# Second block's attention: norms in groups of two tiles, the second half's projections inside the scan, the MLP's norm later

## The chip, the cores and the metric

The kernel runs on one core of one Trainium2 chip. The metric is the device time of one execution in microseconds, lower is better. The core has a matrix engine (TensorE, PE in the profile; its weight loads are PEld), three engines for elementwise work (VectorE is DVE, ScalarE is ACT, GpSimd is POOL) and SyncE (SP), which issues transfers. Each works through its own list of instructions in order and waits on semaphores for the others.

## The reference

Two transformer blocks over x of shape (4, 1024, 256) in float32. Each is "modulated norm, attention, add; modulated norm, feed-forward, add". Block 0 has softmax attention over full rows of 1024 and a low-rank feed-forward; block 1 has the part that the change touches, a causal linear attention with its own MLP inside, and then a mixture layer:

```python
h = _layernorm(x) * (1 + ca) + sa
x = x + ga * _L1_attn_ref(h, ...)      # below
h = _layernorm(x) * (1 + cb) + sb
x = x + gb * _L1_ffn_ref(h, ...)       # 16 tokens share 64 slots

def _L1_attn_ref(inputs, ...):         # 16 heads of 16
    x = layer_norm(inputs, ln1_scale, ln1_bias)
    q, k, v = x @ wq, x @ wk, x @ wv
    phi_q, phi_k = relu(q) + 1e-3, relu(k) + 1e-3
    kv  = cumsum_j(phi_k v^T)          # causal prefix sums
    num, den = phi_q . kv, phi_q . cumsum(phi_k)
    x = (num / den) @ wo + inputs
    y = layer_norm(x, ln2_scale, ln2_bias)
    return x + gelu(y @ w1 + b1) @ w2 + b2
```

## The kernel before

The four sequences are done one after the other by `batch(b, carry)`: four passes of the same instructions. In a pass the 1024 tokens are T = 8 tiles of 128 rows, in two halves of TH = 4 tiles. Nearly all products are float32.

There is no scheduler. Each engine has a `Lane`; `lane.do(emit, *after)` appends a step to that engine's list and notes which steps of other lanes it waits for. So **the order in which the Python code calls `do` is the order on each engine**, and an engine stands still while the next step of its list waits.

The eight PSUM banks go round in `Banks`: `take()` hands out the next bank with the step that last read it, and whoever writes the bank waits for that reader. During block 1's attention one bank (`state_bank`) is set aside and the other seven rotate.

The work around the change, in the order of the code at the end of `batch`:

1. `head_output` ends block 0's attention; `norm_stats` and `norm_apply` normalise each half of x.
2. `feed_rank`, `feed_wide`, `feed_rank2`, `feed_output` are block 0's feed-forward, both halves interleaved.
3. `attention_norms(half, ...)` is a generator with four pieces: statistics of x (L280 to L284), modulation into h (L995, L997), statistics of h, and the apply into xn (L288).
4. `turn` transposes a half (4 tiles by 2 column blocks) on TensorE, and ScalarE copies it out with scale and bias (L411, L418, L420).
5. `attention_inputs` makes keys and values (`wkv1`), queries (`wq1`) and the transposed keys kT of a half; `phi` is L1107 on VectorE; `split_queries` (L1139, ScalarE) writes q_par.
6. The scan runs over t = 0 to 7: `tile_scores` (L1154 on TensorE, then four masks `am` at L1163 on VectorE, 128x512 each), `tile_numerators` (L1181 and, from the second tile, L1185 with kv_state), `tile_state` (L1201, then kv_state at L1209) and `tile_outputs` (L1221, then rec at L1226 and y at L1228).
7. `attention_output(half)` turns y, multiplies by wo, adds to h (L1242), normalises it for the MLP, and leaves three additions and products per tile to GpSimd (L1247 to L1250). Then come `mlp_turn`, `mlp_wide`, `mlp_output`, and the mixture layer (`slot_turn`, `choices`, `chosen_rows`).

A norm of a half is four pairs of bn_stats and bn_aggr, one addition of eps for the four tiles (L283), one power of -1/2 on GpSimd for the four (L284) and four applies (L288) on VectorE.

## Time and profile before

| | |
|---|---|
| three runs | 2003.45, 2004.32, 2004.73 us; median 2004.32 |
| the profiled execution | 2002.16 us |
| its span | 2000.6 us |
| mean granted TensorE clock | 0.959 of full speed |
| busy: PE, DVE, ACT, POOL | 91%, 63%, 44%, 33% |

The span is about four equal passes of some 490 us; the four repeat each other's waits to 0.1 us. The part of a pass that the change touches takes about 120 us. The second pass has it between 771 and 893 us of the span (block 0's norms from 771, the scan from 832 to 893) and the mixture layer's norms up to 970 us. All rows below are of this pass. A granted clock of 1.00 is 2.4 GHz and 0.50 is 1.2 GHz.

### The profile page before, as it was taken

Reading aid. Unit: us, or ns where it says so; the run is one execution under the profiler, and the core shown is the slowest. Engines: PE = TensorE matmul, PEld = TensorE weight load, DVE = VectorE, ACT = ScalarE, POOL = GpSimd, SP = SyncE. Lnnn points to the kernel's source line nnn. Section 1 sums busy time; section 2 is a strip of 40 time slices with the busy share of each in tenths; the row PEclk is TensorE's granted clock in tenths of the full one; section 3 lists DMA queues with packets and bytes.
Section 4 is the critical chain, followed back from the end, with each engine's and each line's share of the span. In section 5 each row is a group of like instructions: output and inputs, shape, how many; then the busy total and the mean of one; then the engine's idle time right before and its main releaser. Section 6 shows DMA issues by size and latency. Waiting matters only on the chain. (4 is left out here: it accounts for less than half of the span.)

```text
span 2000.6 us, 41155 instructions
## 1 busy us (share of the span) xinstructions
PE 1815.9 (91%) x16401; PEld 1287.2 (64%) x16401; DVE 1266.0 (63%) x2699; ACT 887.4 (44%) x1934; POOL 660.6 (33%) x1010
## 2 busy tenths in 40 slices
PE   6999998898999989889899998988989999889888
PEld 4666675656666667566756666756775666765667
DVE  4687846634688883753468887464456888656435
ACT  4566623222467662322257665322135666432222
POOL 2455530120055552012115555201212555420220
PEclk9899998998999999899899999989989999999998
DMA  8566540040266563013136656203114666520400
GB/s 217 124 152 156 138 134 1 2 84 27 77 148 145 140 139 111 1 23 63 33 97 148 144 138 141 85 1 57 29 33 122 142 146 139 118 84 1 85 1 23
DMA packets 128558, 182.64 MB, mean 91 GB/s; under 512 B 33296, under 2 KB 89328, under 8 KB 127344
## 3 DMA queue, kind: packets, MB, share of 16 engines
q1 hardware_dynamic: 114928, 173.72, 36.2%
q10 hardware_dynamic: 13440, 6.30, 1.1%
q8 instruction: 131, 2.15, 0.5%
q14 instruction: 59, 0.48, 0.1%
HBM read 62.44 MB, written 4.24 MB: 33 GB/s over the span
## 5 line engine op out<-in xcount | busy, mean ns | idle before, releaser
L848 ACT ACTIVATE prob<-prob,neg_max 128x768 f32<-128x768 f32 (+5 forms) x384 | 273.8, 715 | 98.4 <-DVE neg_max L740 98.3
L643 PEld LDWEIGHTS bank<-placed,v_t 128*64 128x64 f32 x4608 | 251.2, 137 | 77.7 <-issue 77.7
L623 PE MATMUL scores<-k_t,q_t 64*128 64x128 f32 (+10 forms) x2176 | 291.3, 414 | 0.0
L643 PE MATMUL bank<-placed,v_t 128*64 128x128 f32 x4608 | 274.1, 275 | 17.2 <-DMA placed<-prob 9.7
L284 POOL TENSOR_TENSOR rstd<-rstd,minus_half 128x4 f32<-128x4 f32 x48 | 48.6, 1014 | 713.9 <-DVE rstd L283 713.9
L748 DVE STREAM_TRANSPOSE prob<-prob 128x1536 f32<-128x1536 f32 x128 | 223.7, 1768 | 24.3 <-ACT prob L848 24.0
L810 POOL COPY placed<-prob 32x768 f32<-32x768 f32 x256 | 210.8, 823 | 19.6
L623 PEld LDWEIGHTS scores<-k_t,q_t 64*128 64x128 f32 x2176 | 167.3, 190 | 73.4 <-issue 58.6
L740 DVE CUSTOM_DVE_ANT_1 prob<-scores,hx 128x128 f32<-128x128 f32 (+4 forms) x320 | 166.2, 579 | 59.7 <-PE scores L623 52.3
L797 POOL COPY rec_wide<-rec 128x128 f32<-128x128 f32 x256 | 65.4, 291 | 337.3 <-DVE rec L752 244.3
L848 ACT ACTIVATE hx<-hx,neg_max 128x896 f32<-128x896 f32 (+1 forms) x128 | 119.6, 935 | 83.5 <-DVE neg_max L740 82.8
L740 DVE CUSTOM_DVE_ANT_1 hx<-scores,hx 128x896 f32<-128x896 f32 (+1 forms) x128 | 114.8, 953 | 54.3 <-POOL placed L810 39.6
L748 DVE STREAM_TRANSPOSE hx<-hx 128x1536 f32<-128x1536 f32 x64 | 110.6, 1761 | 13.2 <-ACT hx L848 13.2
L957 DVE TENSOR_TENSOR tmp<-scores,mod_rows 128x256 f32<-128x256 f32 x71 | 30.1, 424 | 125.0 <-PE scores L430 119.1
L810 POOL COPY placed<-hx 32x768 f32<-32x768 f32 x128 | 105.5, 824 | 9.7
L684 PE MATMUL bank<-hT,w_ring 128*128 128x512 f32 x224 | 103.6, 605 | 0.0
L430 PE MATMUL scores<-wout,yT 128*128 128x256 f32 x384 | 90.0, 393 | 7.9 <-POOL yT L819 5.9
L430 PEld LDWEIGHTS scores<-wout,yT 128*128 128x128 f32 x384 | 74.0, 196 | 20.3 <-issue 10.2
L988 ACT ACTIVATE hid<-scores,b 128x512 f32<-128x512 f32 x92 | 60.0, 697 | 52.1 <-PE scores L439 52.1
L1163 DVE TENSOR_TENSOR am<-scores,tril 128x512 f32<-128x512 f32 x96 | 60.2, 683 | 32.2 <-PE bank L1154 19.7
L819 POOL TENSOR_TENSOR yT<-yT,tmp 128x256 f32<-128x256 f32 (+1 forms) x64 | 46.0, 730 | 103.3 <-ACT yT L861 103.3
L740 DVE CUSTOM_DVE_ANT_0 prob<-scores,hx 128x1024 f32<-128x1024 f32 x64 | 75.8, 1222 | 6.6 <-PE scores L623 6.6
(232 smaller groups left out, 3344.8 us busy)
## 6 DMA issues: line engine op xcount, KB each, us to landing
placed<-prob SPq DMA_DIRECT2D x768, 96.0 KB, 2.2
placed<-hx SPq DMA_DIRECT2D x384, 96.0 KB, 2.2
f<-in_L_ffn_f SPq DMA_DIRECT2D x16, 2048.0 KB, 13.5
x<-in_L_attn_x SPq DMA_DIRECT2D x8, 512.0 KB, 4.4
mod_rows<-mod_scratch SPq DMA_DIRECT2D x32, 128.0 KB, 5.7
out<-x SPq DMA_DIRECT2D x16, 256.0 KB, 2.2
w_ring<-in_L_attn_w_q ACTq DMA_DIRECT2D x24, 128.0 KB, 2.5
w_ring<-in_L_attn_w_kv_up ACTq DMA_DIRECT2D x48, 64.0 KB, 2.1
```

Source lines behind the costliest of these rows:

```text
L284: return pool.do(lambda e: nc.gpsimd.tensor_tensor(rstd[:, ts], rstd[:, ts], minus_half[:, ts], op=ALU.pow), var, filled)
L430: last = nc.tensor.matmul(ps, w, m, start=n == 0, stop=n == len(pieces) - 1)
L623: last = nc.tensor.matmul(score_tiles[head][:, at_ // 512, at_ % 512:at_ % 512 + count], q_t[buf][rows_, tile * P:(tile + 1) * P], k_of[bu ...
L643: last = nc.tensor.matmul(out_bank[rows_, at_:at_ + P], v_t[pair % 2][:, j, rows_], placed[m % 2][:, :, head, first_block(m, i) + j, :], s ...
L684: last = nc.tensor.matmul(ps, ring[:, c * P:(c + 1) * P], hT[:, c, cols], start=c == 0, stop=c == C - 1)
L740: nc.vector.tensor_tensor_reduce(prob[m % 3][:, :, head, blocks, :].rearrange("p g n i -> p g (n i)"), src.rearrange("p (g m) -> p g m", g ...
L748: nc.vector.transpose(p_, p_).then_inc(flow["shuffled"], 1)
L797: last = nc.gpsimd.tensor_copy(rec_wide[:, out_slot(m, tile), :].rearrange("p (a n) -> p a n", a=HEADS), rec[:, at_:at_ + HEADS].unsqueeze ...
L810: nc.gpsimd.tensor_copy(placed[m % 2][rows_, g, :, :, :], prob[m % 3][rows_, g, :, :, :]).then_inc(flow["kept"], 1)
L848: nc.scalar.activation(p_, p_, ACT.Exp, scale=-1.0, bias=neg_max[:, k:k + 1], accum_out=row_sum[:, k:k + 1]).then_inc(flow["exp_done"], 1)
L988: return lambda m, cols, ps, done: act.do(lambda e: nc.scalar.activation(dst[:, m, cols], ps, ACT.Gelu_apprx_tanh, bias=bias[:, m:m + 1]), ...
L1163: masked.append(dve.do(lambda e, r=r, ps=ps: nc.vector.tensor_tensor(am[t % 2][:, r * 4:r * 4 + 4, :], ps.rearrange("p (h n) -> p h n", h= ...
```

## The change

**Norms in groups of two.** `norm_stats` now ends each pair of tiles with its own addition and power, and returns for each tile the step that its apply waits for. Every norm of the kernel gets this: one addition and one power of 128x2 more, in place of one of 128x4.

**Turns tile by tile.** `turn` takes both banks first and transposes tile after tile into both, each waiting for its own tile; both copies of ScalarE wait for the last tile.

**The projections.** `attention_inputs` is split: `attention_queries`, `attention_keys` (two tiles) and `attention_keys_turned` (the kT of those two tiles, one bank, one copy). The first half does queries first, then keys 0 and 1, their turn, keys 2 and 3, their turn. The second half's turn and queries come at t = 2, keys 4 and 5 at its end, keys 6 and 7 at t = 3. The fill of v_tok's ones goes from VectorE to GpSimd.

**The second half's norms.** The modulation is now four applies on VectorE (into h) and eight products and additions on GpSimd; statistics of h stand between the masks of tiles 0 and 1, the applies after the masks of tile 1.

**The MLP's norm of the first half.** Its statistics are made in two pieces, at the ends of t = 5 and t = 6, and its applies at the end of t = 6, behind the masks of tile 7, just ahead of `mlp_turn`.

```diff
-        last = None
-        for t, r in zip(tiles or tiles_of(half), ready):
-            s = dve.do(lambda e, t=t: nc.vector.bn_stats(stats[:, t, :], src[:, t, :]), r)
-            last = dve.do(lambda e, t=t: nc.vector.bn_aggr(mv[:, t, :], stats[:, t, :]), s)
-        ts = slice(half * TH, (half + 1) * TH)
-        var = dve.do(lambda e: nc.vector.tensor_scalar(rstd[:, ts], mv[:, ts, 1], eps, None, op0=ALU.add), last)
-        return pool.do(lambda e: nc.gpsimd.tensor_tensor(rstd[:, ts], rstd[:, ts], minus_half[:, ts], op=ALU.pow),
-                       var, filled)
-
-    def norm_apply(src, half, inv, dve=dve):
-        return [dve.do(lambda e, t=t: nc.vector.tensor_scalar(
-            xn[:, t, :], src[:, t, :], mv[:, t, 0:1], rstd[:, t:t + 1], op0=ALU.subtract, op1=ALU.mult), inv)
-            for t in tiles_of(half)]
+        tiles = list(tiles or tiles_of(half))
+        inv = {}
+        for pair, ready_ in zip(zip(tiles[0::2], tiles[1::2]), zip(ready[0::2], ready[1::2])):
+            for t, r in zip(pair, ready_):
+                s = dve.do(lambda e, t=t: nc.vector.bn_stats(stats[:, t, :], src[:, t, :]), r)
+                last = dve.do(lambda e, t=t: nc.vector.bn_aggr(mv[:, t, :], stats[:, t, :]), s)
+            ts = slice(pair[0], pair[1] + 1, pair[1] - pair[0])
+            var = dve.do(lambda e, ts=ts: nc.vector.tensor_scalar(rstd[:, ts], mv[:, ts, 1], eps, None, op0=ALU.add), last)
+            step = pool.do(lambda e, ts=ts: nc.gpsimd.tensor_tensor(rstd[:, ts], rstd[:, ts], minus_half[:, ts], op=ALU.pow),
+                           var, filled)
+            inv.update({t: step for t in pair})
+        return inv
+
+    def norm_apply(src, half, inv, dve=dve, dst=None):
+        dst = xn if dst is None else dst
+        steps = {t: dve.do(lambda e, t=t: nc.vector.tensor_scalar(
+            dst[:, t, :], src[:, t, :], mv[:, t, 0:1], rstd[:, t:t + 1], op0=ALU.subtract, op1=ALU.mult), step)
+            for t, step in inv.items()}
+        return [steps[t] for t in tiles_of(half)]
...
-            copies = []
-            for c in range(C):
-                i, ps, reader = banks.take()
-
-                def transposes(e, c=c, ps=ps):
-                    for t in range(TH):
-                        last = nc.tensor.transpose(ps[:, t * P:(t + 1) * P], src[:, half * TH + t, c * P:(c + 1) * P],
-                                                   ident[:, :])
-                    return last
-
-                done = pe.do(transposes, *ready, reader)
+            copies, taken = [], [banks.take() for c in range(C)]
+            readers = [reader for i, ps, reader in taken]
+
+            def transposes(e, t):
+                for c, (i, ps, reader) in enumerate(taken):
+                    last = nc.tensor.transpose(ps[:, t * P:(t + 1) * P], src[:, half * TH + t, c * P:(c + 1) * P], ident[:, :])
+                return last
+
+            for t in range(TH):
+                done = pe.do(lambda e, t=t: transposes(e, t), ready[t], *readers)
+            for c, (i, ps, reader) in enumerate(taken):
...
-                    h[:, t, :], x[:, t, :], mv[:, t, 0:1], scale, op0=ALU.subtract, op1=ALU.mult), inv)
+                    h[:, t, :], x[:, t, :], mv[:, t, 0:1], scale, op0=ALU.subtract, op1=ALU.mult), inv[t])
...
-            h_done = modulated_rows(half, inv, mod_rows[:, 3, :], mod_rows[:, 2, :])
+            if half == 0:
+                h_done = modulated_rows(half, inv, mod_rows[:, 3, :], mod_rows[:, 2, :])
+            else:
+                h_done = []
+                for t, step in zip(tiles_of(half), norm_apply(x, half, inv, dst=h)):
+                    step = pool.do(lambda e, t=t: nc.gpsimd.tensor_tensor(h[:, t, :], h[:, t, :], mod_rows[:, 3, :],
+                                                                          op=ALU.mult), step, ROWS)
+                    h_done.append(pool.do(lambda e, t=t: nc.gpsimd.tensor_tensor(h[:, t, :], h[:, t, :], mod_rows[:, 2, :],
+                                                                                 op=ALU.add), step))
...
-        def attention_inputs(half, turned, between=iter(())):
-
-
-            if half == 0:
-                ones_set.append(dve.do(lambda e: nc.vector.memset(v_tok[:, :, :, HD1:VPAD], 1.0), turned[0]))
+        def attention_queries(half, turned):
+            q_done[half] = blocks(C, lambda m, cols: [(wq1[:, c, m * P:(m + 1) * P], nT[:, c, cols]) for c in range(C)],
+                                  half, P, lambda m, cols, ps, done: dve.do(phi(qT[:, m, cols], ps), done), turned=turned)
+            return split_queries(half)
+
+        def attention_keys(first, turned):
+
-            for t in tiles_of(half):
+            for t in (first, first + 1):
...
-                next(between, None)
-            q_done[half] = blocks(C, lambda m, cols: [(wq1[:, c, m * P:(m + 1) * P], nT[:, c, cols]) for c in range(C)],
-                                  half, P, lambda m, cols, ps, done: dve.do(phi(qT[:, m, cols], ps), done), turned=turned)
-            kT_done[half] = turn(k_tok, half, k_done, kT)
+            return k_done
+
+        def attention_keys_turned(first, k_done):
+            i, ps, reader = banks.take()
+
+            def transposes(e, t):
+                for c in range(C):
+                    at_ = (c * 2 + t - first) * P
+                    last = nc.tensor.transpose(ps[:, at_:at_ + P], k_tok[:, t, c * P:(c + 1) * P], ident[:, :])
+                return last
+
+            for t, k_step in zip((first, first + 1), k_done):
+                done = pe.do(lambda e, t=t: transposes(e, t), k_step, reader)
+            copy = act.do(lambda e: nc.scalar.copy(kT[:, :, first * P:(first + 2) * P],
+                                                   ps.rearrange("p (c n) -> p c n", c=C)), done)
+            banks.read_by(i, copy)
+            kT_done[first] = kT_done[first + 1] = copy
...
-            half, tok = t // TH, slice(t * P, (t + 1) * P)
+            tok = slice(t * P, (t + 1) * P)
...
-                             kT_done[half][c])
+                             kT_done[t])
...
-        def attention_output(half):
+        def attention_sum(half):
...
-            normed = normalise(h, half, wrote, EPS_LN)
+            return wrote
+
+        def attention_normed(half, inv):
+
+            normed = norm_apply(h, half, inv)
...
+        ones_set.append(pool.do(lambda e: nc.gpsimd.memset(v_tok[:, :, :, HD1:VPAD], 1.0), *rank2_1))
-        attention_inputs(0, attention_turn(0, attn_norm), islice(norms, 2))
-        split = {0: split_queries(0)}
+        attn_turned = attention_turn(0, attn_norm)
+        split = {0: attention_queries(0, attn_turned)}
+        k_first = attention_keys(0, attn_turned)
+        attention_keys_turned(0, k_first)
+        k_first = attention_keys(2, attn_turned)
+        next(norms)
+        attention_keys_turned(2, k_first)
-        attn_norm = next(norms)
+        next(norms)
-            if t + 3 == TH:
-                attn_turned = attention_turn(1, attn_norm)
-            if t + 2 == TH:
-                attention_inputs(1, attn_turned)
-                split[1] = split_queries(1)
+            if t == 2:
+                attn_turned = attention_turn(1, attn_norm)
+            if t == 3:
+                k_first = attention_keys(6, attn_turned)
+                attention_keys_turned(6, k_first)
+            if t == 2:
+                split[1] = attention_queries(1, attn_turned)
+            if t == 0:
+                attn_norm = next(norms)
+            if t == 2:
+                k_first = attention_keys(4, attn_turned)
+                attention_keys_turned(4, k_first)
-                mlp_norms.append(attention_output(0))
+                summed = attention_sum(0)
+            if t == TH + 1:
+                inv = norm_stats(h, 0, summed[0:2], EPS_LN, tiles=(0, 1))
+            if t == TH + 2:
+                inv.update(norm_stats(h, 0, summed[2:4], EPS_LN, tiles=(2, 3)))
+                mlp_norms.append(attention_normed(0, inv))
-        mlp_norms.append(attention_output(1))
+        mlp_norms.append(attention_normed(1, norm_stats(h, 1, attention_sum(1), EPS_LN)))
```

VectorE, between the masks of tile 0 (am0_86) and of tile 1 (am1_78), second pass. Before:

```order
L1163 TENSOR_TENSOR am0_86<-bank1,tril 128x512
L288 TENSOR_SCALAR hx<-hx,mv,rstd 128x256 [waits pool_steps]
L288 TENSOR_SCALAR hx<-hx,mv,rstd 128x256 x3
L1163 TENSOR_TENSOR am1_78<-scores0,tril 128x512 [waits pe_steps]
L1163 TENSOR_TENSOR am1_78<-scores0,tril 128x512 x2
L1163 TENSOR_TENSOR am1_78<-scores1,tril 128x512
L1209 TENSOR_TENSOR kv_state<-scores1,kv_mask 128x272 [waits pe_steps]
```

and now (line numbers are 29 higher there, L1192 is the mask):

```order
L1192 TENSOR_TENSOR am0_86<-bank1,tril 128x512
L282 BN_STATS stats<-hx 128x6 [waits pool_steps]
L283 BN_AGGR mv<-stats 128x2 [waits dve_steps]
L282 BN_STATS stats<-hx 128x6 [waits pool_steps]
L283 BN_AGGR mv<-stats 128x2 [waits dve_steps]
L285 TENSOR_SCALAR rstd<-mv 128x2 [waits dve_steps]
L282 BN_STATS stats<-hx 128x6 [waits pool_steps]
L283 BN_AGGR mv<-stats 128x2 [waits dve_steps]
L282 BN_STATS stats<-hx 128x6 [waits pool_steps]
L283 BN_AGGR mv<-stats 128x2 [waits dve_steps]
L285 TENSOR_SCALAR rstd<-mv 128x2 [waits dve_steps]
L1192 TENSOR_TENSOR am1_78<-scores0,tril 128x512 [waits pe_steps]
```

In place of four applies there are now the statistics of half 1, of which each tile waits for GpSimd; the applies stand behind the masks of tile 1.

VectorE, from the additions to h (L1242) to the masks of tile 6 before; the whole norm stands ahead of them:

```order
L1242 TENSOR_TENSOR hx<-scores0,hx 128x256 [waits pe_steps] x3
L280 BN_STATS stats<-hx 128x6 [waits dve_steps]
L281 BN_AGGR mv<-stats 128x2 [waits dve_steps]
L280 BN_STATS stats<-hx 128x6
L283 TENSOR_SCALAR rstd<-mv 128x4 [waits dve_steps]
L288 TENSOR_SCALAR hx<-hx,mv,rstd 128x256 [waits pool_steps]
L288 TENSOR_SCALAR hx<-hx,mv,rstd 128x256 x3
L1163 TENSOR_TENSOR am0_86<-scores1,tril 128x512 [waits pe_steps]
L1163 TENSOR_TENSOR am0_86<-scores1,tril 128x512
L1163 TENSOR_TENSOR am0_86<-bank0,tril 128x512
L1163 TENSOR_TENSOR am0_86<-bank1,tril 128x512
L1209 TENSOR_TENSOR kv_state<-scores1,kv_mask 128x272 [waits pe_steps]
```

and now, from the kv_state after tile 7's masks to the applies:

```order
L1238 TENSOR_TENSOR kv_state<-scores1,kv_mask 128x272 [waits pe_steps]
L1255 RECIPROCAL rec<-scores0 128x16 [waits pe_steps]
L1257 TENSOR_TENSOR hx<-scores0,rec 128x256 [waits dve_steps]
L282 BN_STATS stats<-hx 128x6
L283 BN_AGGR mv<-stats 128x2 [waits dve_steps]
L282 BN_STATS stats<-hx 128x6
L283 BN_AGGR mv<-stats 128x2 [waits dve_steps]
L285 TENSOR_SCALAR rstd<-mv 128x2 [waits dve_steps]
L293 TENSOR_SCALAR hx<-hx,mv,rstd 128x256 [waits pool_steps]
L293 TENSOR_SCALAR hx<-hx,mv,rstd 128x256
L293 TENSOR_SCALAR hx<-hx,mv,rstd 128x256 [waits pool_steps]
L293 TENSOR_SCALAR hx<-hx,mv,rstd 128x256
```

The norm's second group and its applies stand behind the masks of tile 7 and y of tile 5 (rec, hx).

GpSimd, the powers of the attention's norms. Before:

```order
L1079 TENSOR_TENSOR x<-x,b2_gated_76 128x256 [waits dve_steps] x3
L284 TENSOR_TENSOR rstd<-rstd,minus_half 128x4 [waits dve_steps]
L1079 TENSOR_TENSOR x<-x,b2_gated_76 128x256 [waits dve_steps] x4
L284 TENSOR_TENSOR rstd<-rstd,minus_half 128x4 [waits dve_steps] x5
L1247 TENSOR_TENSOR hx<-hx,b2_1 128x256 [waits dve_steps]
L1248 TENSOR_TENSOR hx<-hx,mod_rows 128x256 [waits pool_steps]
```

and now:

```order
L286 TENSOR_TENSOR rstd<-rstd,minus_half 128x2 [waits dve_steps] x4
L1396 MEMSET v_tok_84 128x128x16 [waits act_steps]
L286 TENSOR_TENSOR rstd<-rstd,minus_half 128x2 [waits dve_steps] x2
L1111 TENSOR_TENSOR hx<-hx,mod_rows 128x256 [waits dve_steps]
L1113 TENSOR_TENSOR hx<-hx,mod_rows 128x256 [waits pool_steps]
L1111 TENSOR_TENSOR hx<-hx,mod_rows 128x256 [waits dve_steps]
L1113 TENSOR_TENSOR hx<-hx,mod_rows 128x256 [waits pool_steps]
```

The fill of v_tok stands straight behind the powers of half 0's two norms, and the modulation of half 1 follows the powers of its own.

## Rows read from the trace of the kernel before

**Rows 1.** The page, its first part: the span.
```profile
span 2000.6 us, 41155 instructions
```

**Rows 2.** Waits of TensorE in one pass, 770 to 1010 us: us, times, longest.
```profile
PE scores L411 <- DVE hx L288: 6.8, 2, 4.0
...
PE scores L439 <- ACT mT L420: 0.4, 1, 0.4
```

**Rows 3.** Timeline of TensorE, 812 to 967 us: start us, us, instruction xcount [idle before].
```profile
815.00 1.06 PE L411 MATMUL scores<-ident,hx 128*128 128x128 f32 x8 [2.79 <-DVE hx L288]
816.49 7.11 PE L439 MATMUL scores<-wkv,nT 128*128 128x512 f32 x12 [0.43 <-ACT nT L420]
...
831.68 0.48 PE L1154 MATMUL scores<-q_par,kT 32*128 32x256 f32 x2 [2.04 <-ACT q_par L1139]
...
864.27 0.48 PE L1154 MATMUL bank<-q_par,kT 32*128 32x256 f32 x2
...
869.30 0.63 PE L411 MATMUL scores<-ident,hx 128*128 128x128 f32 x4 [0.90 <-DVE hx L1228]
...
882.50 0.80 PE L1154 MATMUL scores<-q_par,kT 32*128 32x256 f32 x3 [4.07 <-DVE am L1163]
...
893.32 1.88 PE L439 MATMUL bank<-mT,w 128*128 128x512 f32 x4
```

**Rows 4.** Windows of TensorE: stretch, length, busy (instructions), then its granted clock.
```profile
817.00:820.00 3.00, 3.00 (x5) 0.50 0.01 3
834.00:840.60 6.60, 6.18 (x58) 0.50 0.00 0
882.00:888.00 6.00, 5.50 (x80) 0.50 0.01 3
1003.70:1007.60 3.90, 3.86 (x34) 1.00 0.00 0
```

**Rows 5.** Timeline of VectorE, 802.5 to 882 us.
```profile
802.70 0.42 DVE L280 BATCH_NORM_STATS2 stats<-x 128x6 f32<-128x256 f32 x1
...
806.25 0.48 DVE L995 SCALAR_TENSOR_TENSOR hx<-x,mv,mod_rows 128x256 f32<-128x256 f32 x1 [1.13 <-POOL rstd L284]
...
813.47 1.38 DVE L288 TENSOR_SCALAR hx<-hx,mv,rstd 128x256 f32<-128x256 f32 x4 [1.12 <-POOL rstd L284]
...
818.88 1.76 DVE L1119 MEMSET v_tok<- 128x2048 f32 x1 [0.37 <-issue]
...
835.99 1.37 DVE L288 TENSOR_SCALAR hx<-hx,mv,rstd 128x256 f32<-128x256 f32 x4
837.27 2.48 DVE L1163 TENSOR_TENSOR am<-scores,tril 128x512 f32<-128x512 f32 x4
...
846.80 0.43 DVE L1107 TENSOR_SCALAR k_tok<-bank 128x256 f32<-128x256 f32 x1 [1.00 <-PE bank L439]
...
878.30 2.27 DVE L288 TENSOR_SCALAR hx<-hx,mv,rstd 128x256 f32<-128x256 f32 x4 [1.12 <-POOL rstd L284]
```

**Rows 6.** Timeline of ScalarE, 812 to 860 us.
```profile
815.66 1.45 ACT L420 ACTIVATE nT<-scores,ln_cols 128x512 f32<-128x512 f32 x2 [4.66 <-PE scores L411]
...
855.82 1.07 ACT L418 COPY kT<-bank 128x512 f32<-128x512 f32 x2 [3.04 <-PE bank L411]
```

**Rows 7.** Timeline of GpSimd, 770 to 1012 us.
```profile
812.43 1.01 POOL L284 TENSOR_TENSOR rstd<-rstd,minus_half 128x4 f32<-128x4 f32 x1 [6.21 <-DVE rstd L283]
...
878.79 0.82 POOL L1247 TENSOR_TENSOR hx<-hx,b 128x256 f32<-128x256 f32 x1 [0.53 <-DVE hx L288]
...
887.39 0.73 POOL L1250 TENSOR_TENSOR x<-x,hx 128x256 f32<-128x256 f32 x1
...
1001.99 0.95 POOL L502 MEMSET hx<- 128x1024 f32 x1
```

**Rows 8.** L288 in 1001.5 to 1004.5 us: count, duration ns min/median/max.
```profile
L288 DVE TENSOR_SCALAR hx<-next_x,mv,rstd x4: 394/474/1011, 1002.1 to 1003.8; 128x256 f32<-128x256 f32 x4
```

**Rows 9.** L288 in 813 to 816 us, the same columns.
```profile
L288 DVE TENSOR_SCALAR hx<-hx,mv,rstd x4: 407/408/414, 813.5 to 814.4; 128x256 f32<-128x256 f32 x4
```

## The prediction

> **What bounds the kernel now.** I read the page first: one core, span 2000.6 us [rows 1]; TensorE is busy nine tenths of it, so what counts is where TensorE stands still or runs at the low clock, and what it waits for there. Then the waits of TensorE over one pass, where the largest releaser is the norm's apply (L288) with 6.8 us in two waits [rows 2]. Then the timeline of TensorE through the attention, which names each wait in turn: 2.79 us before the turn of half 0, 2.04 us before the first scores (q_par of ScalarE), 0.90 us before the turn of y, 4.07 us before the scores of tile 7 [rows 3]. Last, windows over stretches behind those waits: behind each of the three long ones the granted clock is 0.50, for 3.0, 6.6 and 6.0 us, that is 1.2 GHz with the engine busy nearly throughout [rows 4]. A wait here is thus dearer than it looks.
>
> The four passes are alike, so I work out one pass and take it four times. The section from the first product on nT (816.49) to the first scores (831.68) is 15.2 us, from there to the scores of tile 5 (864.27) 32.6 us, and from there to the MLP's wide product (893.32) 29.05 us [rows 3].
>
> **A: turns whose tiles are all ready.** ScalarE used to start on the first bank 0.66 us after TensorE began (815.66 against 815.00), after four transposes; eight take 1.06 us [rows 3, 6]. Both copies now wait for all eight: 0.4 us later, and TensorE waits for the copy right behind (0.43 us for nT, 0.4 for mT) [rows 2, 3]. Four turns of a pass are like that (block 0's feed-forward half 0, wo half 1, MLP half 1, mixture half 0): 4 x 0.4 = +1.6 us. The floor is 0, if something else fills the wait. Turns with other work behind them cost nothing.
>
> **B: the mixture's norm of half 1.** TensorE waits 4.0 us for it [rows 2]. A norm loses the idle 1.12 us in front of the applies (0.41 us each alone, four overlapped in 1.38) and pays a second addition, 0.2 us [rows 5, 9]. Applies 0 and 1 take 0.7 us, the second power ends about 1.25 us after its addition began, applies 2 and 3 take 0.7 us: 2.15 us with the extra addition, against 2.5 us. That is 0.4 us, and the last tile has two transposes behind it, not four, another 0.3 to 0.4. B = -0.8 us. I take the second power at the 1.01 us of a 128x4 one [rows 7]; were it half, B gains 0.4 more.
>
> **C: entry to the attention.** The first norm of half 0 loses 1.13 us of idle time wholly, since its applies take 0.92 us a tile, and pays 0.2: -0.9. The second gains as B, -0.4, and the turn -0.3: -1.6 us in all. But GpSimd now fills v_tok right behind the second power. VectorE took 1.76 us for these 2048 elements [rows 5]; GpSimd takes 0.95 us for 1024 [rows 7], so 1.9 us here. The one place where such a fill meets an apply shows 1.011 us for one that takes 0.407 us alone, ending when the fill ends [rows 7 to 9]. Applies 2 and 3 are released at the moment at which the fill starts, so they are held for its 1.9 us. C lies between -1.6 (missed) and +0.3 (held). I take +0.3, since the row shows the hold.
>
> **D: from the product to the first scores.** The 2.04 us for q_par go: queries come first and ScalarE has over 6 us. New are two waits of 0.5 us, as kT is transposed right behind its keys: phi of the last key starts 0.1 us after TensorE and takes 0.43 [rows 5]. All else is the same work. D = -1.0 us, with the low clock at 817 as before; should the gap at C shrink and the clock hold, 3.0 us at half speed give back 1.5 more.
>
> **E: the scan to the scores of tile 5.** Let the first scores start at s. Masks of tile 0 run on VectorE from s+1.2 to s+3.7 (2.48 us for four). Half 1 of h comes from GpSimd in eight instructions that start about s-0.1, after keys 3 and one apply; twelve such stand in 9.3 us (878.79 to 888.12), 0.78 each [rows 7], so the last tile is ready at s+6.2. Its statistics and the addition end at s+7.0 and only then come the masks of tile 1, against s+5.6 before (837.27) [rows 3, 5]. The scores of tile 2 need the banks of tile 1's first two masks: s+8.4, while TensorE is through with tile 0 at s+4.6. It **stands still for 3.8 us**. Then scores 1.15, wait for kv_state until s+10.0, numerators 1.75, state and outputs 1.1; scores of tile 3 wait for three masks of tile 2, which stand behind four applies (1.37): s+13.25. From there TensorE has: scores 1.15, turn 1.0, numerators 1.75, queries 3.44, state and outputs 1.1, keys 3.44, wait 0.5, transposes 0.5, wait 0.7 for the kT copy (one copy is half of the 1.07 us of two, plus its start [rows 6]), scores 1.15, keys 3.44, wait 0.5, transposes 0.5, numerators 1.75, state and outputs 1.1: 22.0 us, so s+35.3. Before it is s+32.6, with 6.6 us of low clock in it. E = +2.7 us. After 3.8 us of rest I expect a low stretch here too, but half of it falls on waits for VectorE; I take 0 for it and keep +2.2 as the upper bound. The lower bound is +0.7: GpSimd doesn't hold the statistics (end at s+6.1) and half of the small waits (2.2 us) are covered; a gain is excluded, since the waits added outweigh the 0.9 us that VectorE could be earlier.
>
> **F: the end of the scan.** Without the norm ahead of the masks of tile 6, the 4.07 us go. Counted from the scores of tile 5, the masks of tile 7 now start at +15.85, after the first group's statistics, and end at +18.35. TensorE finishes y of tile 5 at +17.85 and has only `mlp_turn` next. VectorE still owes kv_state 0.43, rec and y 0.7, the second group's statistics and addition 1.3, and the applies: 2.3 us with GpSimd's additions beside them (878.30: 2.27) and a wait of some 0.4 for the second power. So the last transposes come at +23.8, **5.9 us later**, less six transposes done in between. Then numerators 1.75 and two outputs with a copy, 1.35: +26.9. The low clock follows such a wait: behind 4.07 us it was 6.0 us long, 3.0 us lost [rows 4]; here 1.7 to 3.4, I take 2.45. F = 29.35 - 29.05 = +0.3 us, bounds -2.1 (no low stretch) and +1.3.
>
> **Sum.** 1.6 - 0.8 + 0.3 - 1.0 + 2.7 + 0.3 = +3.1 us a pass, +12.4 us in four. The profiled execution took 2002.16 us, 1.6 us around its span; 2014.6 on that scale. The median is 2.2 us above it: **2017 us**. All other powers and additions lie beside other work: the norms of block 0 under TensorE's head outputs, MLP half 1 under `mlp_output`, next x under the mixture's products. If that cover went, each would cost its 0.2 us.
>
> What the clock does with the transposes now scattered in the waits is open. A stretch of 3.9 us that holds only transposes keeps 1.00, and so do the ones behind it [rows 4]. The Trainium skill, "TensorE: Matmul & The Clock Gate", Part 4 (PE-mode transpose), says that a transpose does not count as the engine being busy in the way a matmul does. By that rule the scattered transposes leave both waits as idle as before, F keeps its low stretch and the rival below with a held clock is gone; by the row they may shorten the rest that the clock sees, and F could come to -2.1. The row decides that transposes can keep a clock, not that six in 5.9 us do.
>
> **Rivals.**
> 1. *The clock holds, faster.* Place: the gap at 812 to 815 and the one before `mlp_turn`. If the fill misses the applies, the first gap is 1.2 us and not 2.8, and if the transposes keep the second from counting, both low stretches go. C = -1.6, D = -2.5, F = -2.1, with 1.6, -0.8 and 2.7 that is -2.7 us a pass: 1993.5 us. It decides only when both stretches go: with the first alone the sum is -0.3. For it: 3.9 us of transposes at 1.00. Against: rows 9, and a gap of 5.9 us where 4.07 was enough to lower the clock.
> 2. *An even exchange.* The fill misses, the first low stretch goes, the end is as forecast: -0.3 us a pass, 2003 us. For it: both start within 0.1 us, and VectorE might be the first.
> 3. *The long low stretch.* The 3.8 us at tile 2 lower the clock for over 6 us as at 834: E = +4.9, F = +1.3, so +6.3 us a pass, 2029.5 us.
> 4. *Groups of two give nothing*, because VectorE's applies wait for the second power as they do for other work of GpSimd: B and C lose 0.5 each, +1.0 us a pass, 2021 us. It lies inside the forecast's range.
>
> **Chances.** Forecast with rival 4: 0.48; rival 1: 0.20; rival 2: 0.20; rival 3: 0.12. About 0.2%, 4 us, is what a measurement of this kernel can tell from no change. Faster than 2000.3 us: rival 1 and a little of 2, 0.22. Between 2000.3 and 2008.3: most of 2, some of the forecast's lower part, 0.17. Slower: 0.61. The forecast's own range is 2009 to 2024 us; with half of each rival's side left out, 1997 to 2027 us.
>
> **What would show it.** In the second pass: the waits of TensorE list the scores behind the masks (am) at tile 2 with 3 to 4 us, and the turn behind the applies before the MLP with 5 us or more. An apply of about 2 us beside the fill of v_tok. The first scores about 0.7 us earlier, the scores of tile 5 about 2 us later, the wide product 2.3 us later, each against 816. The waits behind q_par are gone. The forecast is wrong if the wait at tile 2 is under 2 us (GpSimd or the banks were judged wrong), if the apply beside the fill is 0.4 us, or if windows show 1.00 behind the two gaps.

## The result, and the profile after

| | before | after |
|---|---|---|
| median of 9 runs each, on one chip | 2003.28 us | 2009.26 us (2003.12 to 2014.69) |
| ratio | | 1.0029, 95% interval 1.0015 to 1.0042 |
| span of the profiled execution | 2000.6 us | 2006.5 us |
| mean granted clock | 0.959 | 0.966 |

The change makes the kernel **slower by 0.3%**, 6 us or 1.5 us a pass. The forecast was slower by 12.7 us: the sign was right and the size was twice too large. The page of the kernel after:

```profile
span 2006.5 us, 41185 instructions
PE 1818.7 (91%) x16401; PEld 1280.8 (64%) x16401; DVE 1262.8 (63%) x2727; ACT 890.9 (44%) x1934; POOL 710.1 (35%) x1094
```

TensorE has the same work (16401 instructions in both), and is held up elsewhere. The table cuts a pass at first instructions of TensorE, read from its timeline in all four passes; each number is the mean of four, in us. Two stretches that are equally long in both kernels are left out: 12.2 us from the feed-forward's first output to the end of its last, where the row of C begins, and 8 us between two passes.

| section of a pass | before | after | after, second profile | forecast of the difference |
|---|---|---|---|---|
| block 0's attention with its head outputs | 247.75 | 249.42 | 248.79 | 0 |
| feed-forward (term A) | 15.79 | 16.23 | 16.23 | +0.4 |
| its end to the product on nT (C) | 4.63 | 3.78 | 3.77 | +0.3 |
| product to first scores (D) | 15.06 | 13.26 | 12.84 | -1.0 |
| first scores to those of tile 5 (E) | 32.55 | 36.55 | 35.36 | +2.7 |
| scores of tile 5 to the wide product (F) | 28.97 | 28.63 | 28.39 | +0.3 |
| MLP and mixture to its first product (A, B) | 86.42 | 86.07 | 86.22 | +0.4 |
| to the end of the pass's last combine | 41.37 | 40.24 | 41.65 | 0 |

E is the loss, and C and D give part of it back. The six sections with a forecast sum to +1.1 us a pass in the first profile and to -0.6 in the second. The rest of the difference lies in the first and the last row, which the change hardly touches and which differ between two profiles of the same kernel.

Five of the waits of TensorE over the second pass, kernel after (what waited, for what, us in total, times, longest), which answer to [rows 2]:

```profile
PE scores L416 <- DVE hx L293: 7.0, 5, 3.0
PE bank L1183 <- DVE am L1192: 3.0, 1, 3.0
PE scores L1183 <- DVE am L1192: 1.4, 1, 1.4
PE scores L445 <- ACT mT L426: 0.9, 1, 0.9
PE scores L1183 <- ACT kT L1158: 0.8, 1, 0.8
```

L293 is the apply (L288 before), and its total has not fallen: 7.0 us against 6.8. The wait at the entry fell from 2.79 to 1.57 us and the mixture's from 4.0 to 1.86 and 0.23, but 2.98 and 0.37 us ahead of the MLP's turn are new. The second and third rows are new: scores (L1183) that wait for banks which the masks (L1192) still read. The wait for q_par is gone.

The timeline of TensorE in the attention of that pass, kernel after (start, us, line, tiles; in brackets the idle time ahead and what ended it), answering to [rows 3]:

```profile
812.93 0.76 PE L416 MATMUL scores<-ident,hx 128*128 128x128 f32 x4 [1.57 <-DVE hx L293]
814.56 5.40 PE L445 MATMUL scores<-nT,wq 128*128 128x512 f32 x8 [0.87 <-ACT nT L426]
831.17 1.15 PE L1183 MATMUL scores<-q_par,kT 32*128 32x256 f32 x16 [1.36 <-DVE am L1192]
837.01 0.48 PE L1183 MATMUL bank<-q_par,kT 32*128 32x256 f32 x2 [3.03 <-DVE am L1192]
886.48 1.01 PE L416 MATMUL scores<-ident,hx 128*128 128x128 f32 x4 [2.98 <-DVE hx L293]
887.86 1.49 PE L416 MATMUL scores<-ident,hx 128*128 128x128 f32 x4 [0.37 <-DVE hx L293]
894.12 1.88 PE L445 MATMUL bank<-mT,w 128*128 128x512 f32 x4
```

The 2.79 us in front of the first turn are now the 1.57 us of the first row; the 4.07 us ahead of tile 7 are gone, and 2.98 + 0.37 us stand ahead of the MLP's turn instead. Windows behind the three long waits (PE busy, PEld, DVE, ACT, POOL, granted clock, DMA), answering to [rows 4]:

```profile
815.00:818.80 3.80, 3.80 (x6) 1.49 (x5) 2.60 (x10) 0.30 (x2) 1.38 (x2) 0.55 0.00 0
838.90:842.90 4.00, 4.00 (x67) 3.59 (x59) 3.26 (x8) 0.59 (x1) 0.00 (x0) 0.57 0.02 4
886.10:893.70 7.60, 6.73 (x77) 4.58 (x78) 2.25 (x5) 2.04 (x3) 7.04 (x10) 0.55 0.00 0
```

In this pass TensorE is at 1.2 GHz behind each of them, for 3.4, 3.4 and 6.8 us (the lengths that give these mean clocks).

### The profile page after: what moved, and what is told of

It is laid out like the page before. It is cut to its first block and busy times, and to the rows that moved or that the text cites. A ratio compares the mean times of both kernels' runs of the same rounds, so it can differ in the third digit from the quotient of the medians.

```text
span 2006.5 us, 41185 instructions
## 1 busy us (share of the span) xinstructions
PE 1818.7 (91%) x16401; PEld 1280.8 (64%) x16401; DVE 1262.8 (63%) x2727; ACT 890.9 (44%) x1934; POOL 710.1 (35%) x1094
## 5 line engine op out<-in xcount | busy, mean ns | idle before, releaser
L286 POOL TENSOR_TENSOR rstd<-rstd,minus_half 128x2 f32<-128x2 f32 x96 | 69.7, 726 | 627.1 <-DVE rstd L285 627.1
L416 PE MATMUL scores<-ident,hx 128*128 128x128 f32 x336 | 55.7, 296 | 29.2 <-DVE hx L293 28.1
L445 PE MATMUL scores<-mT,w 128*128 128x512 f32 x176 | 77.9, 594 | 3.5 <-ACT mT L426 3.5
```

Of the source, the lines that this page charges most:

```text
L286: step = pool.do(lambda e, ts=ts: nc.gpsimd.tensor_tensor(rstd[:, ts], rstd[:, ts], minus_half[:, ts], op=ALU.pow), var, filled)
L445: step = pe.do(lambda e, n=n, w=w, m=m: nc.tensor.matmul(ps, w, m, start=n == 0, stop=n == C - 1), copy, *after)
```

## The experiments

Each differs from the kernel after. Its ratio is to the kernel before, timed beside it on the same chip, with a 95% interval in brackets. "Section" means the table above. Two profiles and two sets of runs of one kernel can differ by a pass or two with a low clock, so single edits are judged first by their section, then by the ratio. "Against the kernel after" divides by the ratio 1.0025 of the next experiment.

**The kernel after, once more** (no edit).

> The changed kernel itself, once more, as the yardstick for the others on this chip. If its +0.29% is real, the ratio is 1.002 to 1.004 again. Theory W (waits moved, clock decides the rest): the lengths of the sections that hang on no low clock repeat to 0.1 us (first scores to scores of tile 2 8.35 us, scores of tile 3 to scores of tile 5 22.4 us); the low stretches fall in other passes than in the first profile, so the first scores come 12.4 or 14.1 us after the first product on nT in a pass. Rival N (the difference lies in the unchanged softmax part, 4.8 us of 5.9 in the first profile): that part is again 1 us a pass longer than in the kernel before.

2006.0 us, ratio 1.0025 [1.0010, 1.0040]; its profile is the third column. Here no pass has the low clock behind the wait at tile 2, and three of four have none behind the entry (12.41 us from product to scores, against 14.11 in the other). One low stretch costs 1.7 us in this section. In the scan the low stretch has not vanished: in three of four passes it comes earlier, 2.4 to 2.8 us behind the first scores, and is over before the wait. The wait is then shorter and nothing is lost, since the masks set the time of tile 2. The second pass, where the first scores stand at 826.51:

```profile
834.86 0.48 PE L1183 MATMUL bank<-q_par,kT 32*128 32x256 f32 x2 [1.45 <-DVE am L1192]
```

That is s+8.35 with a wait of 1.45 us, where the first profile has s+8.35 with 3.03. The length of the scan's section thus depends on where the low stretch falls, and that differs between executions of one program.

**The kernel before, once more** (every edit undone).

> The kernel before, once more with a profile, ratio 1.000. It tells how the softmax part, which no edit touches, varies by itself: the first profile of before had it 213.05 us a pass, those of the changed kernel 213.7 to 214.7. If that is chance (where the clock's low stretches fall), it is 214 to 215 here too; if the change lengthens it, it is 213 again.

1.0010 [0.9996, 1.0025]. Differences of 0.1% are nothing here. Its sections differ from the first profile's by up to 0.4 us. The part of block 0's attention ahead of its head outputs takes 213.3 us a pass here and 213.05 in the first profile. In the twelve profiles of changed kernels it takes 213.0 to 214.8 us, in ten of them over 213.5. By the expectation above this speaks for a part that the change lengthens.

**Statistics of h behind the masks of tile 1.**

```diff
-        next(norms)
         mlp_norms, copied, state = [], None, None
...
             if t == 0:
+                next(norms)
+            if t == 1:
                 attn_norm = next(norms)
```

> The statistics of h of half 1 stand behind the masks and kv_state of tile 1, and its applies behind those of tile 2. Theory (the scan loses by the statistics that stand ahead of tile 1's masks and wait for GpSimd): the 3.0 us wait at the scores of tile 2 falls under 1 us, the scores of tile 2 come 2.5 us earlier after the first scores (5.9 instead of 8.35), the low stretch at tile 1 goes; tile 2's masks come 1.1 us later than they could, so of 2.5 + 1.7 us some 2.5 to 3.5 are won: first scores to scores of tile 5 33 to 34 us instead of 36.5; 0.5 to 0.7% faster than the changed kernel. Rival (VectorE bounds the first three tiles whatever the order, the wait only moves to the scores of tile 3): the section stays at 36 us, no change.

1.0008 [0.9995, 1.0021]. TensorE around tiles 2 and 3, in this kernel:

```profile
838.46 0.48 PE L1183 MATMUL bank<-q_par,kT 32*128 32x256 f32 x2 [0.17 <-DVE am L1192]
844.34 0.45 PE L1183 MATMUL scores<-q_par,kT 32*128 32x256 f32 x1 [1.28 <-DVE am L1192]
846.14 1.76 PE L416 MATMUL scores<-ident,hx 128*128 128x128 f32 x8 [0.65 <-DVE hx L293]
```

The 3.03 us become 0.17, and tile 1 to tile 2 takes 3.67 instead of 5.84 us (means of four passes): the statistics ahead of the masks are what held tile 2. But 1.28 and 0.65 us come back at tile 3, where the masks and the turn now wait for the same statistics and applies. From first scores to tile 5 it is 35.43 against 36.55 and 35.36 us, and not the 33 to 34 expected. At either place the norm of half 1 makes VectorE late for TensorE.

**The scan as before**, with everything else of the change.

```diff
-        k_first = attention_keys(2, attn_turned)
         next(norms)
+        k_first = attention_keys(2, attn_turned)
         attention_keys_turned(2, k_first)
-        masked = tile_scores(0, split[0])
         next(norms)
+        masked = tile_scores(0, split[0])
+        attn_norm = next(norms)
...
+            if t == 1:
+                attn_turned = attention_turn(1, attn_norm)
+            if t == 2:
+                k_4 = attention_keys(4, attn_turned)
+                k_6 = attention_keys(6, attn_turned)
+                split[1] = attention_queries(1, attn_turned)
+                attention_keys_turned(4, k_4)
+                attention_keys_turned(6, k_6)
```

(The modulation of half 1 is again VectorE's, by `modulated_rows`; the later places of queries and keys are gone.)

> The second half's work is put back: its modulation on VectorE behind the first keys, its statistics ahead of the masks of tile 0, its turn ahead of the scores of tile 2, its keys, queries and kT in one piece ahead of the scores of tile 3. First half's order, groups of two, turn by tile, the fill and the MLP's norm stay as changed. Theory (the scan's first part lost 3 to 4 us by spreading): first scores to scores of tile 5 falls from 35.4 to 37.4 us to 32 to 33.5; 2.5 to 3.5 us a pass, 0.5 to 0.7% faster than the changed kernel, so about 0.997 against the kernel before. Rival (the spreading costs nothing, the low clock alone makes the difference): this section is 35 us or more.

0.9957 [0.9938, 0.9975]: against the kernel after 0.7% faster. The scan's section is 31.69 us in place of 36.55 or 35.36: **3.7 to 4.9 us a pass is the price of the scan's new order**. The edit takes back three things at once, the spread projections, the modulation on GpSimd and the places of half 1's norm; which of them costs how much is not separated. TensorE's scores of tiles 1 and 2 in this kernel (L1175 is L1183 of the kernel after):

```profile
832.01 1.15 PE L1175 MATMUL scores<-q_par,kT 32*128 32x256 f32 x16 [1.72 <-DVE am L1184]
837.49 1.15 PE L1175 MATMUL scores<-q_par,kT 32*128 32x256 f32 x16 [1.78 <-DVE am L1184]
```

Two waits of 1.7 and 1.8 us, and behind them a long run of products in which VectorE catches up.

**The fill of v_tok behind the norm's last power.**

```diff
-        ones_set.append(pool.do(lambda e: nc.gpsimd.memset(v_tok[:, :, :, HD1:VPAD], 1.0), *rank2_1))
         next(norms)
+        ones_set.append(pool.do(lambda e: nc.gpsimd.memset(v_tok[:, :, :, HD1:VPAD], 1.0), *rank2_1))
```

> The fill of v_tok stands on GpSimd behind the two powers of half 1, where VectorE has no applies. Theory (the fill holds the applies of tiles 2 and 3): these two take 0.73 us instead of 2.18, the first product on nT comes 1.4 us earlier after the feed-forward's output (2.4 instead of 3.8 us), and the wait is short enough that the clock stays at 2.4 GHz in every pass: first scores 12.4 us after it in all four. Together 1.4 to 2.3 us a pass, 0.3 to 0.45% faster than the changed kernel. Rival (the applies are slow for another reason, such as the end of the power): they still take about 2.2 us and nothing changes.

0.9987 [0.9973, 1.0001]. VectorE's applies and GpSimd in the kernel after, then VectorE's applies and TensorE's turn in this one:

```profile
810.03 0.73 DVE L293 TENSOR_SCALAR hx<-hx,mv,rstd 128x256 f32<-128x256 f32 x2
811.02 2.18 DVE L293 TENSOR_SCALAR hx<-hx,mv,rstd 128x256 f32<-128x256 f32 x2 [0.26 <-POOL rstd L286]
808.92 0.69 POOL L286 TENSOR_TENSOR rstd<-rstd,minus_half 128x2 f32<-128x2 f32 x1 [4.09 <-DVE rstd L285]
810.20 0.78 POOL L286 TENSOR_TENSOR rstd<-rstd,minus_half 128x2 f32<-128x2 f32 x1 [0.58 <-DVE rstd L285]
810.93 1.80 POOL L1396 MEMSET v_tok<- 128x2048 f32 x1
```

```profile
812.71 0.73 DVE L293 TENSOR_SCALAR hx<-hx,mv,rstd 128x256 f32<-128x256 f32 x2
813.70 0.74 DVE L293 TENSOR_SCALAR hx<-hx,mv,rstd 128x256 f32<-128x256 f32 x2 [0.26 <-POOL rstd L286]
813.40 1.53 PE L416 MATMUL scores<-ident,hx 128*128 128x128 f32 x8
```

Two applies that take 0.74 us alone take 2.18 beside the fill, and end 0.47 us behind it: the first of them takes 1.86 us and ends 0.15 us behind the fill, the second 0.40. Without the fill there, the turn's eight transposes have no wait that the timeline shows, the section shrinks from 3.78 to 2.34 us, and all four passes go from product to scores in 12.41 us: the low clock behind the entry is gone. Against the kernel after it is 0.4% faster.

**The MLP's turn behind the numerators and outputs of the last tiles.**

```diff
-            else:
-                mlp_turned = mlp_turn(0, mlp_norms[0])
...
+            if t + 1 == T:
+                mlp_turned = mlp_turn(0, mlp_norms[0])
```

> The turn for the MLP stands behind the numerators of tile 7 and the outputs of tile 6, not ahead of them. Theory (TensorE stands still for 3 us and then works at 1.2 GHz although it has work that waits for nothing): the wait shrinks from 3.0+0.4 us to 0.5 or less, no low stretch, so the scores of tile 7 to the wide product take 11.5 to 12.5 us instead of 14.7: 2 to 3 us a pass, 0.4 to 0.6% faster than the changed kernel. Rival (the copy of mT after the turn is now exposed, and y of tile 7 is late for nothing): half of it is lost, 1 us a pass.

0.9964 [0.9948, 0.9981]. The end of the scan on TensorE, this kernel:

```profile
885.98 0.43 PE L1210 MATMUL scores<-am,v_tok 128*32 128x128 f32 x8 [0.85 <-DVE kv_state L1238]
888.36 0.60 PE L416 MATMUL scores<-ident,hx 128*128 128x128 f32 x4
889.49 0.44 PE L416 MATMUL scores<-ident,hx 128*128 128x128 f32 x2 [0.53 <-DVE hx L293]
890.29 0.44 PE L416 MATMUL scores<-ident,hx 128*128 128x128 f32 x2 [0.37 <-DVE hx L293]
891.60 1.98 PE L445 MATMUL bank<-mT,w 128*128 128x512 f32 x4 [0.43 <-ACT mT L426]
```

One wait of 2.98 us becomes small ones of 0.85, 0.53, 0.37 and 0.43, the numerators run at full clock (0.43 us for eight, against 0.65), and the section is 24.42 us in place of 28.63, in all four passes. Against the kernel after it is 0.6% faster.

**The MLP's norm as before**, in one piece at t = 4, with the groups of two.

```diff
-                summed = attention_sum(0)
-            if t == TH + 1:
-                inv = norm_stats(h, 0, summed[0:2], EPS_LN, tiles=(0, 1))
-            if t == TH + 2:
-                inv.update(norm_stats(h, 0, summed[2:4], EPS_LN, tiles=(2, 3)))
-                mlp_norms.append(attention_normed(0, inv))
+                mlp_norms.append(attention_normed(0, norm_stats(h, 0, attention_sum(0), EPS_LN)))
```

> The changed kernel with the MLP's norm of half 0 whole and at the end of tile 4, ahead of the masks of tile 6, as before. Forecast F of the blind text said that the two places are worth the same (+0.3 us for the later one, measured 28.6 against 29.1 us). Theory: the wait before the turn goes and one of 3.4 to 3.8 us at the scores of tile 7 comes with its low stretch; scores of tile 5 to the wide product 28 to 29 us, the whole within 0.15% of the changed kernel. Rival (the later place is a clear gain): 1.5 us a pass slower or more.

1.0022 [1.0005, 1.0039], the same as the kernel after. The wait ahead of tile 7 is back and the one ahead of the turn is gone:

```profile
879.34 0.49 PE L1183 MATMUL scores<-q_par,kT 32*128 32x256 f32 x3 [3.40 <-DVE am L1192]
884.92 1.04 PE L416 MATMUL scores<-ident,hx 128*128 128x128 f32 x8
889.04 1.88 PE L445 MATMUL bank<-mT,w 128*128 128x512 f32 x4
```

The section is 27.25 us against 28.4 to 28.6, but the next one, MLP and mixture, is 87.26 against 86.1 to 86.2, with more of it at the low clock (13.7 us a pass against 6.9 and 10.5). Over the whole kernel, moving the norm behind the masks by itself only moved the wait.

**Norms in groups of four**, with the rest of the change.

```diff
-        for pair, ready_ in zip(zip(tiles[0::2], tiles[1::2]), zip(ready[0::2], ready[1::2])):
+        for pair, ready_ in [(tuple(tiles), tuple(ready))]:
```

> The changed kernel with one addition and one power for all four tiles in every norm but the MLP's of half 0. Theory (a group of two takes the power of the first pair off the path; the power of two columns takes 0.7 us where four took 1.01): entry to the attention 1.3 to 1.6 us longer (both norms of half 0), the mixture's norm of half 1 0.6 us longer, a low stretch behind the entry in more passes; 1.5 to 2.5 us a pass, 0.3 to 0.5% slower than the changed kernel. Rival (the fill holds the last applies anyway, so the groups win nothing at the entry): the entry is longer by 0.9 us at most and the whole under 0.2%.

1.0125 [1.010, 1.015]: against the kernel after 1.0% slower, 5 us a pass, twice what was expected at most. The entry's section is 5.78 us, not 3.78: groups of two are worth 2.0 us there. Behind the longer wait the low clock adds 1.7 us from product to scores (14.95 against 13.25), and MLP and mixture take 0.8 to 1.0 us more. No other part of the change that was taken back alone gains as much. All four applies then wait for one power and meet the fill, and the turn behind them waits 3.18 us:

```profile
820.50 2.83 DVE L293 TENSOR_SCALAR hx<-hx,mv,rstd 128x256 f32<-128x256 f32 x4 [1.12 <-POOL rstd L286]
822.41 1.97 PE L416 MATMUL scores<-ident,hx 128*128 128x128 f32 x8 [3.18 <-DVE hx L293]
```

(Each row is VectorE's and TensorE's timeline of the second pass.)

**The turn bank by bank**, as before.

```diff
-            for t in range(TH):
-                done = pe.do(lambda e, t=t: transposes(e, t), ready[t], *readers)
+                def transposes(e, c=c, ps=ps):
+                    for t in range(TH):
+                        last = nc.tensor.transpose(ps[:, t * P:(t + 1) * P], src[:, half * TH + t, c * P:(c + 1) * P],
+                                                   ident[:, :])
+                    return last
...
+                done = pe.do(transposes, *ready, reader)
```

> The turn is bank by bank again, each waiting for all four tiles; all else as in the changed kernel. Theory (eight transposes ahead of the first copy cost 0.43 us where the tiles are ready, the tile order gains where they come one by one): the stretch from the turn of the feed-forward's half 0 to its output falls from 16.23 to 15.79 us in every pass; wo half 1, MLP half 1 and mixture half 0 give 0.4 each between the wide product and the mixture's first product; against it the entry to the attention and the mixture's half 1 lose 0.3 to 0.5 us each. Net 0.7 to 1.2 us a pass, 0.15 to 0.25% faster than the changed kernel, about 1.001 against the kernel before. Rival (the order of the turn is nothing, the copies hide): under 0.1%.

1.0049 [1.0029, 1.0069], against the kernel after 1.0024: slower, by about as much as the two intervals allow to tell, where a gain of 0.15 to 0.25% was expected. The feed-forward gets its 0.44 us back (15.79), the entry loses 0.7 (4.49) and the end of the scan 0.9 to 1.1 (29.50). MLP and mixture gain 0.4 to 0.6 (85.66). So the turns by tile pay where tiles come one by one, and cost where all are ready.

**Fill and turn together** (the two diffs above).

> The fill of v_tok behind the powers of half 1, and the MLP's turn behind the numerators of tile 7. If the two add up (0.38% and 0.61% alone): 0.9925 to 0.994 against the kernel before; entry to the attention 2.34 us, first scores 12.4 us later, scores of tile 7 to the wide product 10.6 us, in every pass. Rival (part of each gain was the phase of the clock): 0.995 to 0.996.

0.9932 [0.9911, 0.9953]: 2.34, 12.41 and 24.42 us in their sections. Against the kernel after that is 0.9%, and the two alone gave 0.4 and 0.6: the gains add.

**Fill, turn and the scan as before, all three.**

> Three edits in the changed kernel together: second half's work put back as in the kernel before, the fill of v_tok behind the powers of half 1, the MLP's turn behind the numerators of tile 7. Alone they measured -0.68%, -0.38% and -0.61% against the changed kernel. If they add: 0.985 to 0.987 against the kernel before; first scores to scores of tile 5 31.7 us, entry 2.3 us, scores of tile 7 to the wide product 10.6 us, no low stretch behind the entry and the MLP's norm. Rival (the low stretches move to other places): 0.989 to 0.992.

0.9801 [0.9775, 0.9826], 1963.34 us. Four sections together (entry, product, scan, end) take 70.9 us in place of 82.2 (80.4 in the second profile), 9.5 to 11.3 us a pass less, and 1.7 us of them are at the low clock in place of 12.8. The ratios say the same: 0.9801 over 1.0025 is 2.2%, 45 us or 11.2 a pass.

The three edits alone gave 0.4, 0.6 and 0.7% by their ratios, 33 us in sum or 8.4 a pass, each within 0.2%. The difference to 2.2% is barely larger than these intervals allow. In their sections they are worth 2.3, 4.2 and 3.7 to 4.9 us a pass, 10.2 to 11.4 in sum. So the single edits lost some 2 to 3 us a pass elsewhere. Their profiles show some of it: block 0's attention takes 250.0 to 250.3 us a pass in the three of them, with 15.4 to 16.2 us at the low clock, and 248.3 with 12.0 us in this kernel. But each is a single execution, two of them the slowest of their twelve, so how the loss is shared out stays open.

**The same, and each turn in the form that suits it**: by tile where the norm is late, bank by bank where all tiles are ready.

```diff
-        def turn(src, half, ready, dst, scale=None, bias=None, after=None):
+        def turn(src, half, ready, dst, scale=None, bias=None, after=None, by_tile=True):
...
-            return turn(xn, half, normed, mT, scale=ln_cols[:, 2, :], bias=ln_cols[:, 3, :])
+            return turn(xn, half, normed, mT, scale=ln_cols[:, 2, :], bias=ln_cols[:, 3, :], by_tile=half == 0)
```

> As the kernel with the three edits, and the turn goes bank by bank where its tiles are all ready (block 0's feed-forward, wo half 1, MLP half 1, mixture half 0) and tile by tile where they come one by one. Theory (each of four turns pays 0.4 us for the tile order): 1.6 us a pass, 0.3% faster than the kernel with the three edits, 0.982 to 0.984 against the kernel before; the stretch from the feed-forward's turn to its output 15.8 us. Rival (only the first of the four is on the path): 0.1%.

0.9774 [0.9746, 0.9802], 1960.04 us: **2.3% faster than before, 2.5% than the change as made**. The feed-forward is back at 15.80 us. Against the three edits alone (5 and 4 runs) the intervals overlap, so the last step is not shown to pay. Its entry, on TensorE and in a window over it:

```profile
801.16 1.54 PE L418 MATMUL scores<-ident,hx 128*128 128x128 f32 x8
803.56 3.70 PE L460 MATMUL scores<-nT,wq 128*128 128x512 f32 x8 [0.87 <-ACT nT L441]
```

```profile
796.00:806.00 10.00, 8.55 (x54) 5.33 (x55) 9.26 (x34) 1.82 (x3) 2.16 (x3) 1.00 0.00 1
```

Eight products take 3.70 us, where they took 5.40 in the kernel after: the same instructions at 2.4 GHz throughout. In front of them TensorE waits 0.87 us, where it was 1.57 and 0.87. In the four kernels with 0.87 us alone the clock stays up here in all sixteen passes.

## Why the prediction was right in sign and wrong in size

The sections of the table were to sum to +3.1 us a pass in the prediction ("the text" below). They sum to +1.1 in the first profile and -0.6 in the second. Three terms failed: C, the entry, was put 1.15 us too high, because the norm was worth more, the hold cost less, and a low stretch in three passes went; D was put 0.8 to 1.2 us too high, because a clock that holds was counted at nothing; F was put 0.6 to 0.9 too high, because the last transposes of the MLP's turn came earlier. The terms of the MLP and the mixture were 0.6 to 0.8 too high in sum, for reasons that stay open. E alone missed to the other side.

**E, the scan, was right in its mechanism, and is the one large loss.** The forecast was a standstill at tile 2 with scores at s+8.4, the scores of tile 5 at s+35.3, and the last tile of half 1 from GpSimd at s+6.2. Measured with s = 828.66:

```profile
834.08 0.72 POOL L1113 TENSOR_TENSOR hx<-hx,mod_rows 128x256 f32<-128x256 f32 x1
835.51 0.17 DVE L285 TENSOR_SCALAR rstd<-mv 128x2 f32<-128x2 f32 x1
835.59 2.48 DVE L1192 TENSOR_TENSOR am<-scores,tril 128x512 f32<-128x512 f32 x4
```

GpSimd is through at s+6.14, the masks of tile 1 start at s+6.9 (s+7.0 in the text), and the scores of tile 2 come at 837.01, that is s+8.35. The scores of tile 5 come at s+35.36 in the profile where no low clock follows the wait. The wait is 3.03 us where 3.8 stood in the text, since TensorE is through with tile 0 later, at s+5.3. The low clock behind it, taken at 0, comes in three of four passes of the first profile (from tile 2 to tile 3 it is 4.63 us at full clock; measured 5.78, 6.15, 4.63, 6.69) and in none of the second, where it mostly falls ahead of the wait. So E is +2.8 to +4.0; the rival with a long low stretch (+4.9) was half right in one profile.

**C is the step that failed most: +0.3 forecast, -0.85 measured.** The hold itself is shown, by the row of 2.18 us and by the kernel without it. Its size was wrong, and so was that of the norm around it. In the second pass, from which the text worked, the section goes from 4.28 to 3.78 us, and to 2.33 without the hold. The norm and the turn thus gain 1.95 us where the text has 1.6. It took the power of two columns at the 1.01 us of four; the two powers take 0.69 and 0.78, which is enough for the difference. The hold costs 1.45 us where the text has 1.9: two applies at 2.18 instead of 0.74. A third part is in the other passes. The text took all four to be alike, but in three of them the kernel before runs this turn partly at 1.2 GHz (1.94 us for the eight transposes, 1.06 in the second pass) and the section is 4.7 us; the kernel after never does. The Trainium skill, "SBUF — State Buffer", section "SBUF: two separate sides", calls the port pair that VectorE and GpSimd share an exclusive lock that whoever starts first keeps for its whole instruction. The trace agrees: one apply is held until 0.15 us behind the fill, and the next runs at its usual 0.40 us.

**D: -1.0 forecast, -1.8 and -2.2 measured.** The waits went as said. With half of the time at 1.2 GHz taken off, an estimate of the section at full clock, it is 13.5 us before and 12.4 after. The rest is the clock: 3.2 us a pass at 1.2 GHz before, 1.7 and 0.9 after. In two passes of the first profile and three of the second it held (12.41 us). The text had named that and put it at 1.5 more; in the sum it was counted at nothing. The smaller waits behind phi (0.30 us, not 0.5) add a little.

**F: +0.3 forecast, -0.35 and -0.6 measured.** The wait moved ahead of the turn, as said. Counted from the scores of tile 5 (865.55, the wide product less 28.57), the last two transposes come at +23.1, not at +23.8. VectorE's own terms in the text add up to +23.5 for the end of the applies, which come at +23.05, again with a shorter power; the other 0.3 us had no term. Of the 5.2 us between y of tile 5 and these transposes TensorE waits 3.5 (2.98, 0.37 and 0.12) and spends the rest on six transposes, most of them at the low clock. The low stretch is 6.8 us long. From the last two transposes to the wide product it takes 5.5 us where the text's terms at full clock give 3.1, so the low clock costs 2.4 us there, as the text had it (2.45). Only the time of the transposes was wrong. Moving the turn shows that the wait could be avoided: it stood in the program's order, not in the work, which I had counted as unavoidable.

The clock falls at 886.7 us, just behind the start of the first four transposes; over both profiles it falls between 0.5 us before and 2.0 us behind that start. In [rows 4] a stretch of only transposes kept the full clock, and no run here tells what makes the difference. The Trainium skill, "TensorE: Matmul & The Clock Gate", Part 4 (PE-mode transpose), says that a transpose doesn't count as the engine being busy in the way a matmul does; this gap fits it, and [rows 4] does not.

**A and B.** The feed-forward's turn costs +0.44 us (0.4 forecast, and 15.80 again where it is done bank by bank). B by itself is near its forecast: from the start of the last addition to x to the next product on hT it is 5.98 us in place of 7.03 in the second pass, -1.05 (-0.8 forecast). In the MLP and the mixture three turns and the norm come to -0.35 and -0.2 us where their terms sum to +0.4. That section is at the low clock for 9.6 us a pass before, and for 6.9 and 10.5 after, so the clock does not explain both; what does is open.

**The sum, and how much of the sign was luck.** The first profile is 5.9 us longer, 1.5 a pass: +0.44 - 0.85 - 1.80 + 4.00 - 0.34 - 0.35 = +1.1 in the sections with a forecast, the rest in the two others (+1.7 in block 0's attention, -1.1 at the end). The second profile is 2.6 us longer, 0.65 a pass: -0.6 in the sections with a forecast, +1.0 in block 0 and +0.3 at the end. Against the second profile of the kernel before the forecast's sections come to +1.8 and +0.1. So by these sections alone the change is worth between -0.6 and +1.8 us a pass, and the forecast of +3.1 lies outside. That the kernel as a whole came out slower, as forecast, rests in part on block 0's attention, for which the forecast was 0.

The two other sections go with the clock. Block 0's attention with its head outputs has 8.5 and 10.2 us a pass at 1.2 GHz in the two profiles of the kernel before (247.8 and 248.0 us), and 12.0 to 16.2 in all twelve of changed kernels (248.3 to 250.3). Its head outputs take about 33.9 us without a low stretch and 35.5 with one of 3.4 us, in every kernel. The last section has 4.1 us at 1.2 GHz before, and 0.8 and 4.0 after, where it takes 40.24 and 41.65. Why block 0 has more of the low clock in every changed kernel no run here shows.

**The rivals.** *The clock that holds* was right at one of its two places and only in some passes, and not at the other. *The even exchange* had the fill miss the applies, and it didn't. *The long low stretch* is above. *Groups of two give nothing* is refuted by the 2.0 us of the kernel with groups of four. Of the signs that the text asked for these are there: about 3 us behind the masks at tile 2, an apply of about 2 us beside the fill, no wait behind q_par. The wait ahead of the MLP's turn is 3 us and not the 5 or more that the text asked for. One sign of a wrong forecast, a clock of 1.00 behind the first gap, is there in two of four passes.

## What to carry to other kernels

When work is spread to fill one engine's gaps, count the gaps of every engine that works for it: here the projections fitted TensorE, and the norm that feeds them did not fit VectorE between two sets of masks. When a forecast is worked out from one pass, look at the others too: their waits were alike here, and their clocks were not. A wait that moved to another place is often a matter of the order alone; look for steps further down the waiting engine's list that were ready, and put them first (0.6% here). Where short waits each bring a low clock, a low stretch can move to another section when one wait goes, so count the whole kernel beside the section: three edits that gave 0.4, 0.6 and 0.7% alone gave 2.2% together, though that surplus is barely clear of the intervals.
